# Blocks 2 to 15 of the first channel mix take x transposed from DRAM and normalise it there with broadcast rows

## The reference

```python
def _layernorm(x, axis=-1, eps=1e-05):
    m = jnp.mean(x, axis=axis, keepdims=True)
    v = jnp.var(x, axis=axis, keepdims=True)
    return (x - m) / jnp.sqrt(v + eps)

# channel mix
x_prev = jnp.concatenate([jnp.zeros((B, 1, C), x.dtype), x[:, :-1, :]], axis=1)
xr = mu_r * x + (1.0 - mu_r) * x_prev
xk = mu_k * x + (1.0 - mu_k) * x_prev
r = jax.nn.sigmoid(jnp.einsum('btc,dc->btd', xr, W_r))
k = jnp.einsum('btc,dc->btd', xk, W_k)
out = r * jnp.einsum('btc,dc->btd', jnp.square(jax.nn.relu(k)), W_v)

# whole
x = x + 0.5 * ffn(_layernorm(x))
x = x + retention(_layernorm(x))      # q, k, v, chunks with decay, then Wo
x = x + 0.5 * ffn(_layernorm(x))
```

## Time and profile before

| | us |
|---|---|
| median of 3 executions | 339.44 |
| range of the 3 | 339.43 to 340.46 |
| the profiled execution, whole | 338.8 |
| its span (first to last instruction) | 336.9 |
| PE busy | 322.3 |
| DVE busy | 297.0 |
| ACT busy | 210.5 |
| POOL busy | 135.1 |

### The profile page before, as it was taken

How to read it: one execution, slowest core, us unless ns; L and a number is a source line. 1 busy time by engine, 2 the same in 40 slices (tenths; PEclk the granted TensorE clock), 3 DMA queues, 4 the chain that set the end, 5 groups by cost and what they waited for, 6 DMA issues and landing times.

```text
span 336.9 us, 11291 instructions
## 1 busy us (share of the span) xinstructions
PE 322.3 (96%) x4260; PEld 302.4 (90%) x4260; DVE 297.0 (88%) x696; ACT 210.5 (62%) x422; POOL 135.1 (40%) x242
## 2 busy tenths in 40 slices
PE   4979999999999999999999999999999999999975
PEld 4869899999999999999899999989999998989874
DVE  4989899999999999899999989999897979888954
ACT  2877556775757586674758567475857555374362
POOL 4386165608163451706245270715424154221130
PEclk9999999999999999999999999999999999999999
DMA  7610010102001020201102020100000010000001
GB/s 232 247 35 31 4 34 0 34 5 62 4 2 63 2 65 3 65 2 27 41 3 64 2 63 2 53 16 32 2 19 17 2 35 7 26 4 31 34 2 62
DMA packets 11556, 12.08 MB, mean 36 GB/s; under 512 B 1008, under 2 KB 11120, under 8 KB 11504
## 3 DMA queue, kind: packets, MB, share of 16 engines
q1 hardware_dynamic: 11072, 11.18, 10.4%
q10 hardware_dynamic: 432, 0.20, 0.2%
HBM read 7.18 MB, written 4.19 MB: 34 GB/s over the span
## 4 chain that ended last, share of the span: by engine, by line
PE 88%; DVE 4%; issue 3%; ACT 2%; POOL 1%; DMA 1%; ACTq 0%; DVEq 0%; POOLq 0%
PE psum L964 39%; PE psum L956 24%; PE psum L948 7%; PE psum L1035 5%; PE psum L1067 5%; PE psum L1054 3%; PE psum L1025 2%; PE psum L1080 2%; PE psum L1157 1%; DMA ident<-in_ident 1%; ACT xn L344 1%; DVE stats L624 1%; PE psum L1161 1%; PE psum L1127 1%; PE psum L1115 0%
## 5 line engine op out<-in xcount | busy, mean ns | idle before, releaser
L199 POOL TENSOR_TENSOR xr_lo<-xrT,xr_hi 128x512 fp32r<-128x512 f32 x24 | 41.1, 1728 | 99.8 <-ACT xr_hi L375 99.8
L344 ACT ACTIVATE xn<-x,shift,rstd 128x256 f32<-128x256 f32 x96 | 52.0, 591 | 10.1 <-POOL shift L283 10.1
L692 DVE TENSOR_TENSOR attn<-psum,decay 128x512 f32<-128x512 f32 x64 | 42.4, 683 | 4.7 <-PE psum L1035 4.7
L964 PE MATMUL psum<-w_hi,xr_hi 128*128 128x256 f32 x124 | 38.6, 312 | 1.7 <-DVE xr_lo L199 1.2
L624 DVE BATCH_NORM_STATS2 stats<-x 128x6 f32<-128x256 f32 x96 | 35.7, 414 | 4.9 <-DMA x<-in_x 4.6
L276 POOL TENSOR_TENSOR var_eps<-moments,eps 128x2 f32<-128x2 f32 x48 | 18.9, 395 | 43.7 <-DVE moments L628 42.9
L964 PE MATMUL psum<-w_hi,ka_hi 128*128 128x256 f32 x120 | 35.7, 297 | 0.7 <-ACT rgate L403 0.7
L956 PE MATMUL psum<-xa_hi,w_hi 128*128 128x256 f32 x128 | 35.8, 280 | 0.0
L956 PE MATMUL psum<-xk_hi,w_hi 128*128 128x256 f32 x120 | 34.5, 288 | 1.1 <-POOL xk_lo L193 0.9
L956 PE MATMUL psum<-xa_lo,w_hi 128*128 128x256 f32 x128 | 35.5, 278 | 0.0
L956 PE MATMUL psum<-xa_hi,w_lo 128*128 128x256 f32 x128 | 35.5, 277 | 0.0
(11 more groups left out here) (105 smaller groups left out, 1043.4 us busy)
## 6 DMA issues: line engine op xcount, KB each, us to landing
x<-in_x SPq DMA_DIRECT2D x15, 256.0 KB, 2.9
x_out<-y SPq DMA_DIRECT2D x15, 256.0 KB, 3.1
w_f<-in_w SPq DMA_DIRECT2D x7, 256.0 KB, 5.9
decay<-in_decay SPq DMA_DIRECT2D x1, 512.0 KB, 6.6
decq<-in_decq SPq DMA_DIRECT2D x1, 256.0 KB, 6.1
deck<-in_deck SPq DMA_DIRECT2D x1, 256.0 KB, 6.2
x_out<-y SPq DMA_DIRECT2D x2, 128.0 KB, 1.8
x<-in_x ACTq DMA_DIRECT2D x1, 128.0 KB, 2.8
```

The costliest lines, as they stand in the source:

```text
L199: engine.tensor_tensor(xr_lo[f][n % 2][:], xrT[f][n % 2][:], xr_hi[f][n % 2][:].bitcast(F32), ALU.subtract).then_inc(xr_lo_ready[f], 1)
L344: act.activation(xn[s][n % 2][:, t, :], x[n % len(x)][:, t, :], ACT.Identity, bias=shift[s][n % 2][:, t:t + 1], scale=rstd[s][n % 2][:, t: ...
L692: dve.tensor_tensor(attn[r][:], bank[B_SCORES[r]].rearrange("p (g c i) -> p g c i", g=G, c=TILES), decay[:, r, :, :].unsqueeze(2).broadcas ...
L964: mm = pe.matmul(halves(b)[:, t, :], xt[:, g, cols], wt[:, g, :], start=(j == 0), stop=(j == 5))
```

## The change

From block 2 on, FFN1 gets its transposed, normalised input another way.

- The host also passes xT, the transposed x. SP loads 257 columns of it per block (`load_xT`, into a ring of 2), so the token before the block is there too.
- `inverse_std` for FFN1 is as before, but rstd and shift lie in one tile, scale_shift. SP stores both to a DRAM scratch (`store_rows`, two transfers of 256 single elements) and reads them back as rows, broadcast to all 128 partitions (`load_rows`, 2 x 257 elements for each partition).
- POOL forms xnT = xT * rstd row (`scale_xT`) and then + shift row (`shift_xT`), each 128x514.
- ACT makes mu_k * xnT and mu_r * xnT (`scale_k`, `scale_r`, two activations of 128x256 each), and DVE adds (1 - mu) * previous (`mix_k`, `mix_r`, as many instructions as before). `difference` falls away for these blocks, and so do `normalize`, `transpose_T`, `evacuate_T` and `halo`. (1 - mu) is made once by POOL as mu_rest, behind the load of mu.

Three layer norms of single blocks, named in `FAST` (FFN1 block 0, retention block 0, FFN2 block 15), skip the shift: DVE adds eps itself, POOL only takes the power, and DVE subtracts the mean and scales (`normalize_fast`). `warm_up` multiplies a zeroed tile and waits for a memset instead of the identity; 19 instead of 30 of them. PSUM banks are dealt out anew, attn 2 and 3 reuse the space of two f32 weights, and all five programs are in a new order. In the middle of it one round now holds FFN1 of block i, retention of blocks i-2 and i-1 and FFN2 of blocks i-4 and i-3.

```diff
+            def load_xT(n):
+                k = n - FIRST_ROWS
+                sp.wait_ge(xT_scaled, max(k - 1, 0))
+                sp.dma_start(xT[n % 2][:], xT_groups[:, :, n * BT - 1:(n + 1) * BT]).then_inc(xT_loaded[n % 2], 16)
+
+            def store_rows(n):
+                sp.wait_ge(shift_ready[FFN1], shifts(FFN1, n + 1))
+                for k in range(2):
+                    sp.dma_start(rows_out[k, n], scale_shift[FFN1][n % 2][:, k, :], allow_slow_non_contiguous=True).then_inc(rows_stored[n % 2], 16)
+
+            def load_rows(n):
...
+                sp.wait_ge(rows_stored[n % 2], 32 * stored_rows(n))
+                sp.wait_ge(xnT_ready[FFN1], FIRST_ROWS + k - 1 if k > 1 else 0)
+                sp.dma_start(rows[n % 2][:], rows_io[:, n * BT - 1:(n + 1) * BT].partition_broadcast(P)).then_inc(rows_loaded[n % 2], 16)
...
+            load_xT(2)
+            load_w(W_Q)
+            load_w(W_KEY)
+            store_rows(1)
+            load_w(W_VAL)
+            load_w(W_O)
+            store_rows(2)
+            load_table(decq, decq_in, decq_loaded)
+            load_table(deck, deck_in, deck_loaded)
+            load_rows(2)
+            load_table(gstate, gstate_in, gstate_loaded)
+            load_table(decay, decay_in, decay_loaded)
+            load_xT(3)
+            load_xT(4)
+            load_x(4)
...
+            for i in range(8, 16):
+                load_xT(i)
+                store_rows(i - 1)
+                load_rows(i - 1)
+                store_y(i - 8)
+                load_x(i)
...
+                pool.tensor_tensor(xnT[FFN1][n % 2][:], xT[n % 2][:], rows[n % 2][:, 0, :].unsqueeze(1).broadcast_to([P, G, BT + 1]),
+                                   ALU.mult).then_inc(xT_scaled, 1)
...
+                pool.tensor_tensor(xnT[FFN1][n % 2][:], xnT[FFN1][n % 2][:], rows[n % 2][:, 1, :].unsqueeze(1).broadcast_to([P, G, BT + 1]),
+                                   ALU.add).then_inc(xnT_ready[FFN1], 1)
...
+            pool.wait_ge(mu_loaded, 16)
+            pool.tensor_scalar(mu_rest[:], mu[:], -1.0, 1.0, ALU.mult, ALU.add).then_inc(mu_rest_set, 1)
...
+                for g in range(G):
+                    act.activation(akT[n % 2][:, g, :], xnT[f][n % 2][:, g, 1:BT + 1], ACT.Copy, scale=mu[:, 1, g:g + 1]).then_inc(ak_ready, 1)
...
+                    for g in range(G):
+                        dve.scalar_tensor_tensor(out=xkT[f][n % 2][:, g, :], in0=xnT[f][n % 2][:, g, 0:BT], scalar=mu_rest[:, 1, g:g + 1],
+                                                 in1=akT[n % 2][:, g, :], op0=ALU.mult, op1=ALU.add).then_inc(xk_ready[f], 1)
...
+            def normalize_fast(s, n, x):
+                dve.wait_ge(rstd_ready[s], n + 1)
+                dve.wait_ge(xnT_psum[s], max(n - 1, 0))
+                for t in range(TILES):
+                    dve.tensor_scalar(xn[s][n % 2][:, t, :], x[n % len(x)][:, t, :], moments[s][n % 2][:, t, 0:1],
+                                      rstd[s][n % 2][:, t:t + 1], ALU.subtract, ALU.mult).then_inc(xn_ready[s], 1)
...
-            warm_up(3, 14)
+            warm_up(3, 12)
             transpose_T(FFN1, 0)
-            warm_up(3, 13)
+            warm_up(3, 7)
```

1155 lines of the change are left out of this document (625 added, 530 removed).

## The result

The changed kernel takes 506.56 us in the median (499.77 to 515.56), against 339.94 us for the kernel before in the same measurement. The ratio is 1.486, with a 95% interval from 1.479 to 1.493: half as slow again. The forecast was 335.2 us, 1.3% faster, with a range from 331.8 to 340.8.

A forecast was written before the change was run, and what follows sets the result against it. PE's own work was taken to bound the middle, with DVE 6% behind. Terms -6.2 (PE), 0 (middle), +4.0 (start), -2.0 (tail) sum to -4.2: 338.8 to 334.6 us, median 335.2, range 331.8 to 340.8.

The forecast's parts named there:

- What PE loses, 6.2 us: PE, middle rounds: leaving out four transposes saves 0.44 us for each of 14 blocks, 6.2 us; round becomes 18.96 us.
- The middle, 0 us: Middle rounds: DVE, ACT, POOL and row transfers keep up with PE, nothing charged; upper bound 3 us over ten rounds.
- Rival B: Start: two row transfers take mu's 5.4 us instead of about 3, 5 us more on PE: 340.2 us; chance 0.15.
- The start, 4.0 us: Start: new waits for mu and for x of block 4 put PE's retention transposes at 26.35 us; 4.0 us lost.
- The wait for mu, the first of my two: Start: POOL's first power waits for mu until 7.05 us, so first transposes come at 9.15 instead of 7.90.
- C: Middle: DVE becomes the bound as POOL's operations take turns with it, 0.3 us a round: 338.2 us; chance 0.12.
- D: Middle: POOL's scale and shift chain gets on the path, 0.8 us a round, 8.8 us: 344.0 us; chance 0.10.
- The tail, -2.0 us: End: shorter last layer norm brings PE's last transposes from 324.20 to 322.05 us; 2.0 us won, bounds 1.0 and 2.6.
- E: Start: DVE does not stop, rows early or DVE late, so the start costs 1.5 us: 332.7 us; chance 0.18.

The follow-up runs named there:

- the stores turned: Changed kernel with scale and shift transposed on DVE and stored as 16 runs of 128 B instead of single 4 B elements: 347.89 us, ratio 1.026.
- the best one: Start order with x(4) before xT(4), tables behind x(4), mu_rest late, retention block 0 first on DVE and POOL: 344.02 us with DVE-transposed stores, 341.98 without stores.

## Why the prediction was wrong

**What PE loses, 6.2 us: the idea held, the size was too large.** Four transposes fewer in a round were to bring it to 18.96 us; without the stores it is 19.08, so 0.32 us instead of 0.44 (0.28 in the mean of the ten rounds shown below). And I multiplied by 14 blocks, while PE is full, and passes the gain on, in ten or eleven rounds: from the first scores to those of block 13 the kernel without stores wins 3.1 us, all effects together. In the round the new order has one more place where PE changes its kind of work, because `inter` and `intra` no longer stand together; such a seam costs 0.08 to 0.10 us (as from 182.84 to 183.04, 0.20 us where 0.12 is usual). By that estimate it covers most of the gap; no run tests it.

**The middle, 0 us: wrong, and this is nearly the whole result.** The step that failed is the sentence that "the row transfers have some 10 us of a round for what takes two landings". I charged nothing there. The stores cost 164 us in all, some 16 of them ahead of retention's first transposes (43.67 against 27.33 without stores) and the rest in the rounds. I had a landing of 2.5 us for a store, from the rows of x (2.9) and w_f (5.9), transfers of long runs; counted from the issue by 13 us it is even below both. Measured, SP waits 17.6 us for each pair. No row of the trace showed a store of single values, and the nearest in kind that I had, mu, was 128 pieces of 16 B. The experiments with 16 B runs and with padded pieces show why even that was no bound: 16 B runs land in 1.4 us and 4 B pieces 64 B apart in 1.7, while 4 B pieces side by side take 17.6. Rival B had the right operation, but at 5.4 us and at the start alone; I used the landing only for the first rows and gave the other 13 blocks none. Had I worked out from which landing on the store enters SP's loop (some 7.7 us, the estimate above), the forecast would have shown that every us beyond it costs 1 us in each round.

The rule of the Trainium skill that I cited ("DMA: Bandwidth & Descriptors", Rules for kernel authors and Specifications: one descriptor per element, read-modify-write under 512 B) spoke for the right side. The packets agree with one descriptor per element: 30 stores, 7680 pieces, among the 8608 more under 512 B. The page gives no time, and the runs add what it does not say: the pieces are cheap when they lie apart.

**The start, 4.0 us: the chain held, its length did not.** DVE was to stand 2.6 us for x(4) and PE to reach retention at 26.35. In the changed kernel DVE stands 20.75 us and PE gets there at 43.67; it is the same store landing that was mis-sized. With the stores turned it is 8.53 us and 32.08: the rows of block 2, forecast to have landed at 18.5, are only asked for at 18.54, behind two tables of 256 KB, and POOL has them at 25.36. Without stores the number is about right, by luck in parts. DVE stands 0.93 us for x; before that an addition takes it 1.76 us instead of 0.75, beside POOL's shift (20.18 to 21.49), and after it the normalisation 1.65 us, beside a POOL operation on a weight (25.65 to 27.03). PE reaches retention at 27.33 after 4.80 us of waiting, its granted clock is 0.62 over the next 3.7 us, and the first scores start 5.0 us later than before (35.62 against 30.62). The wait for mu, the first of my two, cost little: it ended at 5.72 in the kernel after, not 7.05, and the first transposes came at 7.53, before the 7.90 of the kernel before and not at 9.15.

The turned stores make the kernel another 6.7 us slower in the changed order (347.9 against 341.2) and 2.0 in the best one (344.0 against 342.0); in the first of these the rounds of the middle are 19.08 us as well, so it is lost at the start. Contention between POOL and DVE, which I priced for the middle only (rivals C and D), is part of what the start loses without stores; with the turned stores it is not, since DVE's normalisation takes 0.70 us there and the wait for x is the loss.

**The tail, -2.0 us: not there.** Busy time by stretch, first the kernel before, then the one without stores; the rows begin at the scores of blocks 3, 13 and 15, and the last one goes to the end:

```profile
83.18:276.69 193.51, 193.51 (x2638) 183.55 (x2637) 179.38 (x420) 127.67 (x257) 77.20 (x133) 1.00 0.08 26
276.69:309.94 33.25, 32.68 (x474) 30.41 (x473) 28.41 (x63) 17.80 (x35) 10.81 (x20) 1.00 0.05 17
309.94:336.90 26.96, 20.35 (x263) 18.52 (x262) 17.97 (x40) 12.26 (x27) 4.83 (x8) 0.99 0.09 31
```

```profile
87.86:278.60 190.74, 190.74 (x2601) 181.09 (x2600) 182.38 (x414) 129.86 (x261) 83.56 (x150) 1.00 0.18 48
278.60:313.49 34.89, 34.80 (x486) 32.22 (x485) 29.29 (x65) 17.70 (x36) 10.21 (x20) 1.00 0.05 17
313.49:340.20 26.71, 20.87 (x263) 18.83 (x262) 18.72 (x41) 11.91 (x26) 4.95 (x4) 1.00 0.09 31
```

The first row of each spans ten rounds, 19.35 us each before and 19.07 now. Behind that it is 61.6 us against 60.2: the last stretch is only 0.25 us shorter, and the one before has 12 matmuls more, work that the new order has put off to there. The shorter chain before the last transposes exists (13.77 us from the scores of block 15 instead of 14.26), worth a quarter of what I had, since PE reached it with work in hand and the steps behind the transposes did not move up.

**The account of the kernel without stores**, in spans, against before: +5.0 at the first scores, -3.1 from there to block 13 (at 278.60 it is 1.9 behind), +1.4 behind: +3.3, which is 340.2 - 336.9.

**The rivals.** C and D did not come: PE is full in the middle in spite of POOL's work. E did not come. The result is one that none of them held: the dearest, D, added 8.8 us, and the only one on the stores, B, took its landing from the same few rows.

What stays open: why neighbouring 4 B pieces cost so much, and whether the change can win at all. The ten variants that were measured several times reach 1.005 to 1.026 of the kernel before, and the five of them that use the real scale and shift 1.016 to 1.026. A version that keeps the old way for blocks 2 and 3, and so the old start, could keep some of the 0.32 us per round (at most 3 to 4 us, an estimate); it was not tried.

## What to carry to other kernels

A small transfer is not cheap because it is small: before one is put into a loop, find its landing time in a trace, or measure it, in its own shape (piece size and distance in memory), and work out how long it may take until the loop is as long as the round. If single values from many partitions must go to DRAM, runs of 16 B or pieces 32 to 64 B apart were cheap here and neighbouring pieces of 4 B were not; what is issued behind a slow store in the same queue is late too, waited for or not. Where the order at the start is reshuffled, follow each of PE's next two inputs through every engine, and count POOL's large operations against DVE's.

## What the runs showed of the hardware

- 512 pieces of 4 B stored side by side by two transfers kept the waiting queue for 17.6 us, and what was issued straight behind them without a wait landed after 19 us; 4, 8, 16, 32 and 64 B apart the same pieces take 18.4, 6.5, 3.9, 2.6 and 2.1 us from first issue to the end of the wait; one transfer of 128 runs of 16 B lands in 1.4.
- A load of 257 KB in which all 128 partitions read the same 2 KB lands in 5.0 us, one of as many bytes from different rows in 3.5 in the same place, and xT, the same load elsewhere in the round, in 2.8.
- Two DVE operations of 128x256 took 0.73, 1.68 and 2.62 us beside no, one and two POOL operations of 128x514.
- After 6.8 us without matmuls PE's granted clock was 0.50 for the 3.5 us that follow. It was 0.50 for 4.8 us after two stops of 1.4 and 3.2 us with only four transposes between them, and stayed at 1.00 after one of 1.2 us.
